# The experts' products of a routed layer: fp32 matrix products replaced by three products of fp16 high and low parts, with both weights split by GpSimd during the attention

## The reference

```python
for e in range(E):                                   # E = 8, D = 256, I = 1024
    h = _layernorm(hidden_states, ln_g[e], ln_b[e])
    h = gelu(einsum('bld,di->bli', h, w1[e]) + b1[e])      # exact gelu
    h = einsum('bli,id->bld', h, w2[e]) + b2[e]
    out = out + combine[..., e:e + 1] * h            # zero but for the two chosen experts
x = _layernorm(x + out, axis=-1)
```

## Time and profile before

| | us |
|---|---|
| median of 3 runs | 3234.8 (3231.3 to 3237.1) |
| span of the profiled execution | 3232.2 |
| experts: first W1 copy to start of the last scatter | 2673.1 to 3198.6 |
| one expert tile in between, u to u | 7.25 |
| last scatter to the end | 33.6 |

### The profile page before, as it was taken

One profiled execution on the slowest core, in us unless ns is written; L12 is line 12 of the kernel. 1 busy time (PEld: TensorE's weight loads), 2 busy tenths in 40 slices (PEclk: granted clock), 3 DMA queues, 4 the chain that ended last, 5 costly groups with the idle time before them and its releaser, 6 DMA issues. The chain is left out here.

```text
span 3232.2 us, 72457 instructions
## 1 busy us (share of the span) xinstructions
PE 3089.3 (96%) x29281; PEld 1389.4 (43%) x29282; DVE 2735.8 (85%) x2902; ACT 2502.6 (77%) x4689; POOL 453.2 (14%) x654
## 2 busy tenths in 40 slices
PE   8999999999999999999999999999999969999995
PEld 4333333333333333333333333333332658999995
DVE  3599999999999999999999999999998683433443
ACT  3269999999999999999999999999999552333333
POOL 2000000000000000000000000000000464555554
PEclk9989999999999999999999999999999979999997
DMA  6520101111020101011010101021002561222224
GB/s 159 124 45 15 35 21 30 30 34 28 15 35 24 28 15 35 29 30 28 28 28 18 34 21 28 15 51 28 15 9 83 206 227 34 38 38 36 36 37 124
DMA packets 101213, 152.92 MB, mean 47 GB/s; under 512 B 21592, under 2 KB 64464, under 8 KB 99248
## 3 DMA queue, kind: packets, MB, share of 16 engines
q1 hardware_dynamic: 85008, 130.03, 16.2%
q0 software_dynamic: 15904, 18.66, 3.6%
HBM read 88.35 MB, written 60.29 MB: 46 GB/s over the span
## 5 line engine op out<-in xcount | busy, mean ns | idle before, releaser
L1005 DVE TENSOR_REDUCE half_max<-scores 128x2 f32<-128x1024 f32 x2016 | 2297.4, 1219 | 10.5 <-PE scores L759 4.8
L930 ACT ACTIVATE probs<-bank 128x512 f32<-128x512 f32 x4012 | 2142.3, 595 | 142.5 <-PE bank L772 45.5
L831 PE MATMUL bank<-probs,V 128*32 128x256 f32 x16384 | 1309.6, 391 | 44.2 <-ACT probs L930 42.4
L759 PE MATMUL scores<-K,Q 48*128 48x512 f16 x4032 | 793.9, 388 | 3.0 <-SPq L542 2.2
L772 PE MATMUL bank<-Q,K 50*128 50x512 f16 x4012 | 789.7, 380 | 0.0
L831 PEld LDWEIGHTS bank<-probs,V 128*32 128x32 f32 x16384 | 322.5, 108 | 583.2 <-issue 517.7
L759 PEld LDWEIGHTS scores<-K,Q 48*128 48x128 f16 x4032 | 194.2, 93 | 834.6 <-DVE half_max L1005 532.2
L772 PEld LDWEIGHTS bank<-Q,K 50*128 50x128 f16 x4012 | 371.2, 94 | 183.0 <-ACT probs L930 4.2
L660 POOL TENSOR_SCALAR max_parts<-row_max 128x16 f16<-128x16 f32 x64 | 16.2, 253 | 2066.3 <-DVE row_max L1011 2066.3
L1604 ACT ACTIVATE h<-u 128x1024 f32<-128x1024 f32 x71 | 75.0, 1057 | 260.8 <-DVE u L1648 260.8
L1565 PE MATMUL pre<-xgT,w 128*128 128x128 f32 x2272 | 265.3, 275 | 2.3 <-ACT xgT L1598 2.3
(11 more groups left out here) (195 smaller groups left out, 1204.8 us busy)
## 6 DMA issues: line engine op xcount, KB each, us to landing
attended<-att SPq DMA_DIRECT2D x64, 256.0 KB, 2.5
W<-in_L_ffn_w_dram SPq DMA_DIRECT2D x16, 1024.0 KB, 6.4
Q<-q_parts SPq DMA_DIRECT2D x96, 128.0 KB, 6.6
K<-k_parts SPq DMA_DIRECT2D x96, 128.0 KB, 6.9
values<-attended SPq DMA_DIRECT2D x6, 2048.0 KB, 9.2
q_parts<-parts SPq DMA_DIRECT2D x64, 128.0 KB, 2.4
k_parts<-parts SPq DMA_DIRECT2D x64, 128.0 KB, 2.4
xT<-in_x_cols_dram SPq DMA_DIRECT2D x8, 512.0 KB, 4.9
```

What stands on the lines that cost most here:

```text
L759: mm = nc.tensor.matmul(scores[:, b, h, :], Q[p][r, c, up, t * P:(t + 1) * P], K[p][r, up, kc * TC:(kc + 1) * TC], start=True, stop=True)
L831: mm = nc.tensor.matmul(banks[att_bank[s // KB]][32 * u:32 * u + 32, q], V[wp][:, wk, u // 2, :], probs[:, 4 * s % RING + u, q], start=(wk ...
L930: nc.scalar.activation(probs[:, i % RING, :], banks[tile_bank[i]][:], ACT.Exp, scale=SCALE).then_inc(exp_done, 1)
L1005: nc.vector.tensor_reduce(half_max[lc % 2][:, :, up, t, kc], scores[:, b], AX.X, ALU.max).then_inc(max_done[b], 1)
```

## The change

Both expert weights and both left operands become a high fp16 part and a low one (value minus high part). A product is then the sum of three fp16 products, high by high, high by low and low by high, in the same PSUM accumulation; the low by low product is dropped. Powers of two lift the values (16 for the rows, 256 for the weights) and are taken out again in the gelu's scale and in the second bias. GpSimd makes the parts of the weights in the attention, in 32 pieces of 128 x 1024, one every other chunk: load, three GpSimd instructions, and for W1 a store into `w1_parts` in memory. ScalarE makes the high parts of the rows (`x_high`) and of the gelu's output (a second gelu that writes fp16), VectorE the low parts (`x_low`, `h_low`). In `step` everything ahead of the W2 product is one tile further ahead than before: W1's product, bias and gelu are for n + 2, rows are turned and normed for n + 3, gathers run for n + 5, and the indices of one tile are copied per tile instead of four at once.

```diff
+ROW_LIFT = 2.0 ** 4
+W_LIFT = 2.0 ** 8
+W_PARTS = ((0, 0), (0, 1), (1, 0))
...
+    w1d = nc.dram_tensor("w1_parts", (E, P, KD, 2, I), F16, kind="Internal").ap()
...
-        W2 = top.enter_context(nc.sbuf_tensor("W2", [P, E, IC, D], F32))
+        W2 = top.enter_context(nc.sbuf_tensor("W2", [P, E, IC, 2, D], F16))
...
-        W1 = top.enter_context(nc.sbuf_tensor("W1", [P, E, KD, I], F32))
+        W1 = top.enter_context(nc.sbuf_tensor("W1", [P, E, KD, 2, I], F16))
...
+            def load_piece(n):
+                if n >= 1:
+                    sp.wait_ge(w_made, n)
+                if 1 <= n <= W1_PIECES:
+                    sp.dma_start(w1d[(n - 1) // KD][:, (n - 1) % KD], w_cut).then_inc(w1_stored, 16)
+                if n < W1_PIECES:
+                    sp.dma_start(w_raw, w1[n // KD].rearrange("(k p) i -> p k i", p=P)[:, n % KD]).then_inc(w_loaded, 16)
+                else:
+                    e, b = (n - W1_PIECES) // 2, (n - W1_PIECES) % 2
+                    sp.dma_start(w_raw.rearrange("p (c d) -> p c d", d=D),
+                                 w2[e].rearrange("(c p) d -> p c d", p=P)[:, HC * b:HC * (b + 1)]).then_inc(w_loaded, 16)
...
-                    if lc == CH + 2:
-                        sp.dma_start(W2[:, bass.ds(it, 1)].rearrange("p o c d -> p (o c) d"),
-                                     w2.rearrange("e (c p) d -> e p c d", p=P)[it]).then_inc(w2_loaded, 16)
+                    if lc % 2 == 0:
+                        load_piece((it * RC + lc) // 2)
...
+            def cut_weights(n):
+                pool.wait_ge(w_loaded, 16 * (n + 1))
+                if n < W1_PIECES:
+                    raw, high, low = w_raw, w_cut[:, 0], w_cut[:, 1]
+                    if n >= 1:
+                        pool.wait_ge(w1_stored, 16 * n)
+                else:
+                    e, b = (n - W1_PIECES) // 2, (n - W1_PIECES) % 2
+                    raw = w_raw.rearrange("p (c d) -> p c d", d=D)
+                    high, low = (W2[:, e, HC * b:HC * (b + 1), w, :] for w in range(2))
+                nc.gpsimd.tensor_scalar(raw, raw, W_LIFT, None, ALU.mult).then_inc(w_cutting, 1)
+                pool.wait_ge(w_cutting, 2 * n + 1)
+                nc.gpsimd.tensor_copy(high, raw).then_inc(w_cutting, 1)
+                pool.wait_ge(w_cutting, 2 * n + 2)
+                nc.gpsimd.tensor_tensor(low, raw, high, ALU.subtract).then_inc(w_made, 1)
...
+                    if lc % 2 == 1:
+                        cut_weights((it * RC + lc) // 2)
...
+                if k == 0:
+                    dve.wait_ge(w_made, PIECES)
+                    dve.wait_ge(w1_stored, 16 * W1_PIECES)
...
-                sp.dma_start(W1[:, e], w1[e].rearrange("(k p) i -> p k i", p=P)).then_inc(w1_loaded, 16)
+                sp.dma_start(W1[:, e], w1d[e]).then_inc(w1_loaded, 16)
...
-            nc.scalar.copy(ln_cols[:].rearrange("p w e k -> p (w e k)"), turned[:, 0:LR])
-            nc.scalar.copy(b1c[:].rearrange("p e c -> p (e c)"), turned[:, LR:LR + BR])
+            nc.scalar.activation(ln_cols[:].rearrange("p w e k -> p (w e k)"), turned[:, 0:LR], ACT.Copy, scale=ROW_LIFT)
+            nc.scalar.activation(b1c[:].rearrange("p e c -> p (e c)"), turned[:, LR:LR + BR], ACT.Copy,
+                                 scale=ROW_LIFT * W_LIFT)
...
-    XB = 4
-    FAR = XB - 1
+    FAR = 5
+    HELD = GB - 1
...
             def step(n, it, q, left):
                 if left >= FAR:
-                    if not isinstance(n, int) or n > 0:
-                        pool.wait_ge(turned, n)
-                    pool.wait_ge(ys_ready, n + 2)
-                    if q % XB == XB - FAR:
-                        pool.wait_ge(cur_ready, it + 2)
+                    if later(n, GB - FAR):
+                        pool.wait_ge(turned, n + FAR - GB + 1)
+                        pool.wait_ge(ys_ready, n + FAR - GB + 3)
+                    if later(n, 3):
+                        pool.wait_ge(cur_ready, n - 1)
                     pool.sem_inc(gate, 1)
                     gather(n + FAR, (q + FAR) % GB)
-                if not isinstance(n, int) or n > 0:
+                if later(n, 1):
                     pool.wait_ge(added, 16 * n)
+                if left >= HELD and later(n, 1):
+                    nc.gpsimd.tensor_copy(cur[:, (q + HELD) % GB:(q + HELD) % GB + 1, :],
+                                          routes[:, bass.ds(n + HELD, 1), :]).then_inc(cur_ready, 1)
                 pool.wait_ge(ys_ready, n + 3)
                 pool.sem_inc(gate, 1)
-                nc.gpsimd.indirect_dma_start(x1d, bass.IndirectOffsetOnAxis(ap=cur[q // XB][:, q % XB, 1:2], axis=0),
+                nc.gpsimd.indirect_dma_start(x1d, bass.IndirectOffsetOnAxis(ap=cur[:, q, 1:2], axis=0),
                                              ys[q % 2][:], None, compute_op=ALU.add).then_inc(added, 16)
-                if q % XB == 0 and left >= XB:
...
             def times_w1(n, p):
                 pe.wait_ge(w1_ready, n + 1)
-                pe.wait_ge(xgT_ready, KD * (n + 1))
+                pe.wait_ge(x_low_ready, n + 1)
+                if later(n, 2):
+                    pe.wait_ge(u_ready, n - 1)
                 for c in range(IC):
                     for k in range(KD):
-                        mm = nc.tensor.matmul(pre[p][:, c, :], w1[p][:, k, c * P:(c + 1) * P],
-                                              xgT[p][:, k * P:(k + 1) * P], start=(k == 0), stop=(k == KD - 1))
+                        for i, (wp, rp) in enumerate(W_PARTS):
+                            mm = nc.tensor.matmul(pre[p][:, c, :], w1[p][:, k, wp, c * P:(c + 1) * P],
+                                                  xp[p][:, rp, k * P:(k + 1) * P], start=(k == 0 and i == 0),
+                                                  stop=(k == KD - 1 and i == len(W_PARTS) - 1))
                 mm.then_inc(pre_ready, 1)
             def step(n, it, q, left):
                 p = q % 2
-                if left >= 1:
-                    if not isinstance(n, int) or n > 0:
-                        pe.wait_ge(u_ready, n)
-                    times_w1(n + 1, 1 - p)
+                e = owner(pe, n)
+                if left >= 3:
+                    turn_rows(n + 3, it + (q + 3) // GB, (q + 3) % GB)
                 if left >= 2:
-                    turn_rows(n + 2, it + (q % XB + 2) // XB, (q + 2) % XB)
-                e = owner(pe, n)
-                pe.wait_ge(h_ready, n + 1)
+                    times_w1(n + 2, p)
+                pe.wait_ge(h_low_ready, n + 1)
                 pe.wait_ge(y_ready, n + 1)
                 for c in range(IC):
-                    mm = nc.tensor.matmul(py[p][:, 0:D], h[p][:, c, :],
-                                          W2[:, bass.ds(e, 1), c, :], start=(c == 0), stop=(c == IC - 1))
+                    for i, (hw, wp) in enumerate(((0, 0), (1, 0), (0, 1))):
+                        mm = nc.tensor.matmul(py[p][:, 0:D], hp[p][:, hw, c, :], W2[:, bass.ds(e, 1), c, wp, :],
+                                              start=(c == 0 and i == 0), stop=(c == IC - 1 and i == 2))
                 mm.then_inc(py_ready, 1)
...
+                act.wait_ge(xgT_ready, KD * (n + 1))
+                if later(n, 2):
+                    act.wait_ge(pre_ready, n - 1)
+                nc.scalar.copy(xp[p][:, 0, :], xgT[p][:]).then_inc(x_high_ready, 1)
             def gelu(n, p):
                 act.wait_ge(u_ready, n + 1)
-                nc.scalar.activation(h[p][:], u[:], ACT.Gelu).then_inc(h_ready, 1)
+                if later(n, 2):
+                    act.wait_ge(h_low_ready, n - 1)
+                nc.scalar.activation(h[p][:], u[:], ACT.Gelu, scale=1.0 / (ROW_LIFT * W_LIFT))
+                if later(n, 2):
+                    act.wait_ge(py_ready, n - 1)
+                nc.scalar.activation(hp[p][:, 0], u[:], ACT.Gelu, scale=1.0 / (ROW_LIFT * W_LIFT)).then_inc(h_high_ready, 1)
...
+                if left >= 3:
+                    norm_rows(n + 3, 1 - p)
                 if left >= 2:
-                    norm_rows(n + 2, p)
+                    gelu(n + 2, p)
                 weigh(n, it, q)
...
-            def take_w1(n, p, used):
+            def take_w1(n, p):
                 e = owner(dve, n)
-                if used is not None:
-                    dve.wait_ge(pre_ready, used)
-                nc.vector.tensor_copy(w1[p][:], W1[:, bass.ds(e, 1), :, :].rearrange("p o k i -> p (o k) i")
+                if later(n, 2):
+                    dve.wait_ge(pre_ready, n - 1)
+                nc.vector.tensor_copy(w1[p][:], W1[:, bass.ds(e, 1)].rearrange("p o k w i -> p (o k) w i")
                                       ).then_inc(w1_ready, 1)
-            def add_b1(n, p, used):
+            def x_low(n, p):
+                dve.wait_ge(x_high_ready, n + 1)
+                nc.vector.tensor_tensor(xp[p][:, 1, :], xgT[p][:], xp[p][:, 0, :], ALU.subtract).then_inc(x_low_ready, 1)
+            def add_b1(n, p):
```

(30 more changed lines are left out.)

141 lines of the change are left out of this document (76 added, 65 removed).

## The result

The changed kernel takes 3147.8 us in the median of 4 runs (3145.0 to 3149.8), beside 3233.1 us (3229.5 to 3237.1) for the kernel before. The ratio is 0.9737, with a 95% interval of 0.9725 to 0.9748.

A forecast was written before the change was run, and what follows sets the result against it. Attention bound by VectorE, experts by TensorE, after the change by the ScalarE-VectorE ring at 6.40 us per tile: 68 x (7.245 - 6.40) = 57.5, less 2 at the start, plus 3.7 at the end, 55.8 off: 3179 us, range 3160 to 3228.

The forecast's parts named there:

- weighing to norm: Ring term on ScalarE: from the weighing's start to the norm, owner read in between, 0.96 us.
- the ring: Experts: ScalarE and VectorE steps from bias through gelus, weighing, norm, cast and `x_low` to the next bias, 6.35 us per tile.
- `x_low` to bias: Ring term on VectorE: from `x_low`'s start to the bias, owner read in between, 0.86 us.
- added for GpSimd's lock: Experts: 0.05 us per tile added to the ring for a copy that finds GpSimd at work.
- TensorE 5.50: Experts: TensorE's products and row turns per tile would take 5.50 us, against 7.25 before.
- GpSimd 5.8 to 6.3: Experts: GpSimd's scatter, gathers and index copy per tile, if a whole copy of W1 falls in: 5.8 to 6.3 us.
- Start: Experts up to the third bias: 2 us less, bounds -4 and +4.
- End: Experts from last bias to last scatter: 13.3 us where 9.65 before, so 3.7 more.
- Attention 0: Attention: GpSimd's making of the weight parts lies beside VectorE's work, priced at 0, bound +3.
- TensorE stays the bound: Rival: the ring has slack through owner reads that run ahead; 5.6 us a tile, 3125 us, chance 0.08.
- GpSimd hinders: Rival: GpSimd and VectorE hinder each other in part, delaying the ring; 6.6 to 7.1 a tile, 3193 to 3227, chance 0.20.
- The slower one: Rival: GpSimd becomes the bound, held up by `h_low` too; 7.56 a tile, 3258 us, chance 0.12, half-speed copy included.

The follow-up runs named there:

- e1: Changed kernel with ScalarE norming every tile by expert 0's scale and bias, so no owner read ahead of the norm: 3131.3 us, ratio 0.9682.
- e3: Changed kernel with one line moved: VectorE adds the bias of tile n+2 ahead of `x_low` of n+3: 3118.2 us, ratio 0.9643.
- e6: Changed kernel with W1's third product left out, 16 of 48 instructions: 3146.2 us, ratio 0.9728.
- e2: Changed kernel with the first gelu's `h` written to PSUM, so `h_low` has one SBUF input: 3149.0 us, ratio 0.9734.
- e8: Changed kernel with VectorE adding expert 0's bias to every tile, so no owner read between `x_low` and bias: 3129.3 us, ratio 0.9682.
- e9: Changed kernel with GpSimd making the high and low part of each weight piece four times: 3147.3 us, ratio 0.9740.
- e5: Changed kernel with bias ahead of `x_low`, `h` in PSUM and all tiles laid out without the hardware loop: 3119.8 us, ratio 0.9648.

## Why the prediction was right in direction and wrong in size

**The step that failed** is the term "weighing to norm" of the ring, 0.96, "owner read included". It took the distance of gelu and norm in the earlier trace rows, with an owner read in between, for what a read costs, whatever stands ahead of it. But 0.96 is the spacing of a gelu and what follows it, read or no read: in the kernel after, gelu to gelu is 0.96 with none in between. The read is done by ScalarE's sequencer, which is free once the weighing has been handed over, and that happens when `y` is ready, while the second gelu still runs. The trace has it so. In the loop tile above `y` ends at 2905.77 and the second gelu at 2906.23; the read of the owner begins at 2906.02, before the weighing starts at 2906.14:

```profile
L1534 ACTq TENSOR_LOAD <-owner_i x1: 277/277/277, 2906.0 to 2906.0; - x1
```

The norm starts 0.81 behind the start of that read. Outside the loop the read begins 0.10 behind the end of `y`, and `y` mostly ends 0.48 ahead of the weighing, so the norm can start 0.40 behind the weighing, which is its distance without any read. So outside the loop the read is mostly covered wholly (0.40, and hardly a change there in e1); in the loop in part (0.69 in the tile shown, 0.40 once it is gone).

The whole difference in the tile shown, 6.40 forecast against 5.95:

| step | forecast | measured |
|---|---|---|
| bias to gelu, gelu to gelu, gelu to weighing | 3.18 | 3.17 |
| weighing to norm | 0.96 | 0.69 (0.40 outside the loop) |
| norms | 0.79 | 0.84 |
| cast and hand-over | 0.56 | 0.43 |
| `x_low` to bias | 0.86 | 0.82 |
| added for GpSimd's lock | 0.05 | 0.00 |

The step to the norm accounts for 0.27 of 0.45, the cast and its hand-over for 0.13. On average over the trace's rings the steps are 3.19, 0.64, 0.84, 0.44 and 0.88, so the tile shown stands for the rest. Over 68 tiles 0.45 are 30 us, of a miss of 33.2 between the two profiled executions (89.0 measured, 55.8 forecast) and of 29.5 between the medians; the profiled one of the change is the fastest of its four. What the other 3 us are stands under start and end below.

**The rest, point by point.**
- *The ring becomes the bound*: right. e3 opens it and gains 29.6; e6 takes 0.9 from TensorE and e2 takes 0.7 from GpSimd, and both gain nothing.
- *TensorE 5.50*: 5.52 in e3. Products by W1 start 0.056 apart in the middle of its tiles, those by W2 0.109. The Trainium skill (TensorE: Matmul & The Clock Gate, Back-to-back issue gap), by whose 81 ns the sum was 6.70, does not hold for these pairs: with 0.081 e3's tile could not be 5.52.
- *`x_low` to bias, with the owner read in it*: right, 0.82 against 0.86, and e8 shows 0.48 of it to be the read.
- *GpSimd 5.8 to 6.3*: near what the packed chain took beside the ring, 5.96, but no bound: it fits into 5.52 in e3, where its busy time in 2850 to 3000 is 4.7 a tile and not 5.3.
- *The copy of W1 keeps its 1.23*: right, 1.22 in the middle; up to 1.43 in the tiles where it meets GpSimd's indirect DMAs.
- *Start*: third bias at 2693.35 against 2696.28 before, 2.9 less where 2 were forecast. That is luck: the first copy of W1 itself began 2.6 earlier, within the spread of such times, and from there to the third bias it took 22.9 against 23.2, 0.3 less. *End*: last bias to last scatter, 3098.21 to 3111.64, is 13.4 against 13.3 forecast:

```profile
3098.21 1.22 DVE L1719 TENSOR_TENSOR u<-pre,b1c 128x1024 f32<-128x1024 f32 x1
...
3111.64 1.56 POOL L1576 DMA_INDIRECT x<-ys,cur  x1 [2.93 <-DMA x<-ys,cur]
```

- *Attention 0*: right (e9). *Last 33.6 us*: 31.6 now, 2 less. From the last issue of an output transfer to the last instruction are 3.3 us, in all twelve traces of changed kernels, for 5.4 in the one of before; why is open.
- *Sum in the traces*: 68 x (7.245 - 5.954) = 87.8, + 2.9 - 3.8 + 2.1 = 89.0, the difference of the spans (3232.2 and 3143.2).

**The rivals.** "TensorE stays the bound" named the right mechanism, owner reads that run ahead, but gave it to all reads: it holds for ScalarE's and not for VectorE's. "GpSimd hinders" was half right: GpSimd is held up, by more than the sum said, but that did not reach the ring. The slower one (GpSimd as the bound, at 7.56 a tile) named a real cause, `h_low` with two SBUF inputs, and gave it too much: the packed chain stayed at the ring's period. The Trainium skill (SBUF — State Buffer, Who interferes with whom) has such an instruction contend with GpSimd's reads, and infers that making descriptors needs the write side; what the prediction drew from that, that the gathers would lose little, is not borne out: GpSimd is busy 0.72 less per tile once an input is in PSUM (e2), and the shares' gather beside `h_low` takes 0.95 in e5 and 1.35 in the kernel after.

The range failed because the ring's own bounds, 6.25 to 6.60, treated the read as certain; the range's lower end, 3160, lay only 9 us below the 3169 of these bounds. The rival at 3125 stood at 0.08, and what lies in between, a read that is covered on one engine and not on the other, had no case of its own.

## What to carry to other kernels

A distance between two instructions measured where a read lies between them is not the price of the read: ask what the sequencer had handed over by then, and whether the engine ahead was still busy. A ring of two engines can be opened cheaply, by moving the step that waits for another tile's chain behind the one that feeds the next long stage; here that one move added a third to the gain of the whole change. When two chains have the same period in a trace, free one: if the period stays and the freed engine begins to wait, it had only followed; if the period falls, it was the bound.
